# Moving stores, weight loads and mask making of a graph kernel out of the preparation of its tile tables into its first edge sum

## The reference, cut to what matters

```python
edge_index = jnp.stack([src, dst])
h = jnp.maximum(_layernorm(x), 0.0)
x = x + L0(h, edge_index, edge_weight, ...)   # weighted graph convolution and a 2-layer head
...                                           # L1: graph convolution
...                                           # L2: three typed attention layers
...                                           # L3: attention with edge attributes

def L0(h6, edge_index, edge_weight, W, b, W1, b1, W2, b2):
    row, col = edge_index                     # self-loops of weight 1 are appended to both
    deg = segment_sum(ew_sl, row_sl)
    norm = rsqrt(deg)[row_sl] * ew_sl * rsqrt(deg)[col_sl]
    msgs = (h6 @ W)[col_sl] * norm[:, None]
    h7 = segment_sum(msgs, row_sl) + b
    return relu(h7 @ W1 + b1) @ W2 + b2
```

## Time and profile before

| | us |
|---|---|
| median of 3 runs (range) | 5548.44 (5533.56 to 5564.57) |
| profiled execution, its own time | 5535.18 |
| span of the profile | 5533.5 |
| first SP issue of `load_pairs` | 174.28 |
| first SP issue of `spread_sum` | 207.99 |
| first and last start of an indirect addition (L867) | 221.1 and 1088.0 |
| first SP issue of `between_sums` | 1093.54 |

### The profile page before, as it was taken

The page is one execution under the profiler, slowest core; times in us unless marked ns, Lnnn a source line. Parts: engine busy times, 40 slices in busy tenths (PEclk is TensorE's granted clock), DMA queues, the critical chain, the costliest instruction groups (busy, mean ns, idle before and its releaser), DMA issues. The chain is left out here.

```text
span 5533.5 us, 69081 instructions
## 1 busy us (share of the span) xinstructions
PE 4208.4 (76%) x19341; PEld 3323.8 (60%) x19341; DVE 3814.4 (69%) x8692; ACT 1622.2 (29%) x3882; POOL 3333.5 (60%) x3108
## 2 busy tenths in 40 slices
PE   4666666377777678887987888798788878878886
PEld 4554445254444566666886666688666667756665
DVE  6644444275555569998436999853699986679998
ACT  3443334230000432222443222234322223422221
POOL 2388888717777467774136777513677750067775
PEclk9888888689999889998998999999899999989998
DMA  4488888736666577786027787612787762077775
GB/s 159 102 123 124 124 122 124 112 118 209 211 212 210 169 236 240 238 242 190 23 73 235 241 244 238 199 32 73 224 245 237 238 188 67 17 220 235 233 239 171
DMA packets 525140, 959.77 MB, mean 173 GB/s; under 512 B 87701, under 2 KB 299875, under 8 KB 523954
## 3 DMA queue, kind: packets, MB, share of 16 engines
q0 software_dynamic: 224512, 549.90, 39.6%
q1 hardware_dynamic: 300130, 404.93, 22.9%
q10 hardware_dynamic: 128, 0.52, 0.0%
HBM read 718.56 MB, written 236.50 MB: 173 GB/s over the span
## 5 line engine op out<-in xcount | busy, mean ns | idle before, releaser
L1462 POOL DMA_INDIRECT L2a_rows<-kv_rows,typed_index x960 | 957.8, 998 | 292.5 <-issue 292.5
L1767 PE MATMUL L2a_sums<-L2a_weighted,L2a_hot 128*128 128x264 f32 x2784 | 791.1, 430 | 204.6 <-DVE L2a_weighted L1617 174.5
L867 POOL DMA_INDIRECT sum_rows<-L0s_rows,L0s_row_of x464 | 726.8, 1566 | 153.7 <-issue 119.3
L1756 PE MATMUL L2a_query<-x,L2a_turned 128*128 x2784 | 727.9, 408 | 50.5 <-ACT L2a_turned L1711 27.8
L1767 PEld LDWEIGHTS L2a_sums<-L2a_weighted,L2a_hot 128*128 128x128 f32 x2784 | 555.3, 209 | 347.8 <-DVE L2a_weighted L1617 199.1
L1756 PEld LDWEIGHTS L2a_query<-x,L2a_turned 128*128 128x128 f32 x2784 | 568.4, 207 | 152.5 <-issue 56.5
L1286 POOL DMA_INDIRECT L1s_rows<-rows,index x464 | 451.1, 972 | 270.4 <-ACTq L87 129.2
L1462 POOL DMA_INDIRECT L3a_rows<-feature_rows,index x464 | 480.9, 1037 | 154.9 <-issue 154.9
L1002 PE MATMUL L0s_message<-features,L0s_share 128*128 x928 | 314.9, 498 | 292.4 <-ACT L0s_share L967 292.4
L1462 POOL DMA_INDIRECT hold<-kv_rows,typed_index x432 | 429.0, 993 | 178.4 <-issue 178.4
L2298 POOL TENSOR_SCALAR L2d_here<-hold,mask 128x256 f32<-128x256 f32 x200 | 183.1, 934 | 537.8 <-DVE hold L2374 389.7
(11 more groups left out here) (428 smaller groups left out, 8319.0 us busy)
## 6 DMA issues: line engine op xcount, KB each, us to landing
code_rows<-L1s_code SPq DMA_DIRECT2D x232, 256.0 KB, 2.9
L3a_code<-code_rows SPq DMA_DIRECT2D x116, 512.0 KB, 4.0
L0s_wide<-source_rows SPq DMA_DIRECT2D x116, 256.0 KB, 3.9
L2a_turn<-turned_rows SPq DMA_DIRECT2D x87, 256.0 KB, 4.4
L2a_pens<-mask_rows SPq DMA_DIRECT2D x87, 256.0 KB
L2a_hot<-hot_rows SPq DMA_DIRECT2D x87, 256.0 KB, 3.9
kv_rows<-L2d_key_rows SPq DMA_DIRECT2D x50, 384.0 KB, 2.6
kv_rows<-L2d_value_rows SPq DMA_DIRECT2D x150, 128.0 KB, 2.4
```

The lines of the kernel that those rows point to most:

```text
L867: pool.indirect_dma_start(c.sum_rows[u], bass.IndirectOffsetOnAxis(ap=row_of[:, 4 * n + u:4 * n + u + 1], axis=0), rows[n % ring][:, u, :] ...
L1462: pool.indirect_dma_start(rows[n % ring][:, u, :], None, table, bass.IndirectOffsetOnAxis(ap=index_of[:, t:t + 1], axis=0)).then_inc(lande ...
L1756: last = pe.matmul(query[q % 2][:, u, :], turned[quad % 2][:, u, :], at(c.q, b[2 * q + u // 2]), start=True, stop=True)
L1767: last = pe.matmul(sums[(m * WP + j) % held][:, :], hot[quad % 2][:, j % 2 * 2 + k, :], weighted[:, 2 * j + k, :], start=k == 0, stop=k == 1)
```

## The change

The four attribute fields are copied by GpSimd instead of ScalarE, into a free part of the accumulator `c.acc`. VectorE clips the source indices first. The key's transposes and the edges' first and last keys are only copied to `c.acc`; masks and links are made from them in `spread_sum`, after quads 4 to 8 of VectorE's loop. SyncE's loads of weights and its stores of fields follow the first eight `wide` loads of `spread_sum`, its store of masks follows quad 11, and their landing is waited for at the end of that stage.

```diff
-def load_pairs(nc, c, copies):
+def load_pairs(nc, c):
...
         def _(sp):
-            for to, source in copies:
-                sp.dma_start(to, source).then_inc(stored, 16)
             sp.wait_ge(clipped_ready, 1)
             sp.dma_start(c.source_rows...)
-            sp.wait_ge(split, 1)
-            for f in range(4):
-                sp.dma_start(c.field_rows[f, :, :]..., fields[:, f, :, :]).then_inc(stored, 16)
-            sp.wait_ge(filled, 1)
-            sp.dma_start(c.mask_rows...)
-            sp.wait_ge(stored, 16 * (6 + len(copies)))
+            sp.wait_ge(stored, 16)
...
+            dve.tensor_scalar(clipped[:, :, :], ...).then_inc(clipped_ready, 1)
             dve.tensor_copy(ends[:, 0, :], ...)
             dve.tensor_copy(ends[:, 1, :], ...)
-            dve.tensor_scalar(clipped[:, :, :], ...).then_inc(clipped_ready, 1)
-            dve.memset(masks[:, :, :, :], -FAR)
-            dve.memset(apart[:, :, :], 1.0)
-            dve.memset(c.links[:, :], 0.0)
...
-            ...  (L532 to L547: copies, four differences, five masks, links)
+            dve.tensor_copy(c.origin, origin_ps)
+            dve.tensor_copy(c.start, first_ps[:, :])
+            dve.tensor_copy(c.tail, last_ps[:, :])
+            dve.tensor_copy(c.key_t, key_ps[:, :, :])
...
         def _(act):
-            for f in range(4):
-                last = act.activation(fields[:, f, :, :], c.raw[:, :, :, 4 + f], ACT.Copy)
-            last.then_inc(split, 1)
...
+        def _(pool):
+            for f in range(4):
+                pool.tensor_copy(c.fields[:, f, :, :], c.raw[:, :, :, 4 + f])

-def spread_sum(nc, c, name):
+def spread_sum(nc, c, name, copies):
...
             for n in range(wides):
                 load_wide(n)
+            for to, source in copies:
+                sp.dma_start(to, source).then_inc(kept, 16)
+            for f in range(4):
+                sp.dma_start(c.field_rows[f, :, :]..., c.fields[:, f, :, :]).then_inc(kept, 16)
             for n in range(quads):
+                if n == 3 * ring:
+                    sp.wait_ge(masked, 1)
+                    sp.dma_start(c.mask_rows...).then_inc(kept, 16)
                 sp.wait_ge(packed, n + 1)
                 sp.dma_start(c.hot_rows[:, own], hot8[n % 2][:, :])...
...
+            sp.wait_ge(kept, 16 * (5 + len(copies)))
...
                 tally(2 * n + 1, blocks[2 * n % 8 + 1])
+                if n == 2 * ring - 4:
+                    differ_inside()         # memset of masks, one difference, two masks
+                if n == 2 * ring - 3:
+                    differ_from(2, 0)       # one difference, one mask
+                if n == 2 * ring - 2:
+                    differ_from(3, P - 1)   # one difference, one mask
+                if n == 2 * ring - 1:
+                    mark_origin()           # the fifth mask
+                if n == 2 * ring:
+                    link()                  # two memsets, two differences, links
```

More of the change, by code:

```diff
@@ L531, in _ @@
             dve.tensor_copy(c.heads[:, :], heads_ps)
[L532 to L542, removed]
-                              ALU.is_equal).then_inc(filled, 1)
-            dve.tensor_tensor(apart[:, 1:, 0], first_ps[:, 1:], tail[:, 0:NT - 1], ALU.not_equal)
-            then(dve.tensor_tensor(apart[:, :, 1], first_ps[:, :], tail[:, :], ALU.not_equal))
-            dve.tensor_scalar(c.links[:, 0:2 * NT], apart[:, :, :].rearrange("p t s -> p (t s)"), -FAR, None, ALU.mult)
-            dve.tensor_scalar(c.linked[:, :], apart[:, 0::WT, 0], -1.0, None, ALU.add)
+            dve.tensor_copy(c.origin, origin_ps)
+            dve.tensor_copy(c.start, first_ps[:, :])
+            dve.tensor_copy(c.tail, last_ps[:, :])
+            dve.tensor_copy(c.key_t, key_ps[:, :, :])
         @block.tensor
@@ L850, in spread_sum @@
         hot_stored, turn_stored = ([st.sem(f"{x}{s}") for s in range(2)] for x in ("hot_stored", "turn_stored"))
+        framed, masked, kept = (st.sem(x) for x in ("framed", "masked", "kept"))
         wide_landed = [st.sem(f"wide_landed{s}") for s in range(wides)]
@@ L933, in tally, with then, differ_inside, differ_from @@
                 dve.tensor_tensor(to, to, number[:, j:j + 1], ALU.add).then_inc(counted, 1)
+            count = [0]
+            def then(instruction):
+                count[0] += 1
+                instruction.then_inc(framed, 1)
+                dve.wait_ge(framed, count[0])
+            def differ_inside():
+                dve.memset(c.masks[:, :, :, :], -FAR)
+                then(dve.tensor_tensor(c.differ[:, :, 1:], c.key_t[:, :, 1:], c.key_t[:, :, 0:P - 1], ALU.not_equal))
+                dve.tensor_scalar(c.masks[:, :, 0, 1:], c.differ[:, :, 1:], -FAR, None, ALU.mult)
+                then(dve.tensor_scalar(c.masks[:, :, 1, 0:P - 1], c.differ[:, :, 1:], -FAR, None, ALU.mult))
+            def differ_from(k, e):
+                then(dve.tensor_tensor(c.differ, c.key_t, spread(c.key_t[:, :, e], 2, P), ALU.not_equal))
+                then(dve.tensor_scalar(c.masks[:, :, k, :], c.differ, -FAR, None, ALU.mult))
+            def mark_origin():
+                dve.tensor_tensor(c.masks[:, :, 4, :], spread(c.count[0:CH, :], 1, 4), spread(c.origin, 2, P),
+                                  ALU.is_equal).then_inc(masked, 1)
+            def link():
+                dve.memset(c.links[:, :], 0.0)
+                then(dve.memset(c.apart, 1.0))
+                dve.tensor_tensor(c.apart[:, 1:, 0], c.start[:, 1:], c.tail[:, 0:NT - 1], ALU.not_equal)
+                then(dve.tensor_tensor(c.apart[:, :, 1], c.start, c.tail, ALU.not_equal))
+                dve.tensor_scalar(c.links[:, 0:2 * NT], c.apart.rearrange("p t s -> p (t s)"), -FAR, None, ALU.mult)
+                dve.tensor_scalar(c.linked[:, :], c.apart[:, 0::WT, 0], -1.0, None, ALU.add)
             for s in range(hots):
```

37 lines of the change are left out of this document (20 added, 17 removed).

## The result

The changed kernel is slower: 5564.60 us as the median of 14 runs (5555.17 to 5576.86), against 5549.26 us for 14 runs of the kernel before. The ratio is 1.0031, with a 95% interval of 1.0020 to 1.0042, that is 17 us more by a ratio and 15 by the medians, where 12 us less was forecast. The profiled execution took 5562.49 us, its span is 5560.9.

What follows compares the result with a forecast made beforehand. The prediction took GpSimd's additions to bound the first sum and a store's landing to end the preparation. Its terms, -22.4 + 10.3 = -12.1 us, took 5548.4 to 5536.3 us, range 5514 to 5553.

Steps and rivals of the forecast that it cites:

- The preparation (-22.4 us): Stage before the first sum: ends with VectorE's copy at 185.2 us, so the sum starts 22.4 us earlier (15.9 to 22.4).
- S: Start of the first sum, at its first `wide` load: 207.99 us before, 185.6 forecast.
- as the sum had it: The prediction's total of its terms, not the kernel's stage: -22.4 + 10.3 = -12.1 us.
- Ten transfers ahead of the byte store (+10.3 us): Start of the first sum: quad 0's byte stores queue behind weights and fields, GpSimd waits 10.3 us (3.6 to 18.3).
- The masks behind quad 11 (0): First sum: the masks' store delays quad 12's byte stores, but ScalarE's lead of about three quads covers it, costing nothing.
- The starved rival: First sum: SyncE's queue starves beside additions, fields cost 18.3 us and masks 18; 14 us slower, 5562; chance 0.07.
- Masks on VectorE inside the sum (0): First sum, quads 4 to 8: some 11 us of masks and links lie under VectorE's 422.0 us of waiting, costing nothing.
- GpSimd: four copies ... hidden under VectorE: Preparation: GpSimd's four field copies take 7.3 us, end at 181.7 before VectorE, and cost nothing.
- The forecast's own test: End of the first sum: GpSimd's last addition starts some 12 us earlier; forecast wrong if under 4 or over 19.

Runs made afterwards that it cites:

- the spread versions: Changed kernel, fields on ScalarE, moved transfers issued one at a time at every second quad from quad 12: 0.9974 with stores cut into 112 and 4, 0.9994 undivided.

## Why the prediction was wrong, point by point

**The preparation (-22.4 us): the mechanism held, the size was 19.2 by S.** VectorE's copy of the keys ends the stage, as the sum had it, but ended at 188.6 and not at 185.2. Of the 3.4 us, 0.83 are an earlier stage that ended later in this execution (VectorE starts at 175.16 instead of 174.33), and 2.75 are VectorE slowed by GpSimd's copies; together a little over the 3.4. (The first addition gained 19.8, since it starts 12.5 us behind S and not 13.1.) The sum took GpSimd's copies as harmful only if they ended last. They were shorter than the 7.3 us taken (5.14), and cost more by what they did beside them.

**Ten transfers ahead of the byte store (+10.3 us): right, and 7.3 us.** GpSimd restarted at S + 27.6, not S + 31.2; the wait for the store and its place were as forecast, and 7.3 lies within the bounds of 3.6 and 18.3.

**The masks behind quad 11 (0): wrong, about 7 us.** The step counted ScalarE's lead of three quads as a cover. But each addition also waits for the one four before it, whatever ScalarE has in hand, and beside the masks additions landed after up to 10.6 us instead of 6.9. (That both meet on the masks' four engines is argued, not shown.) The starved rival had the place and a price of 18 us, but by the wrong wait, the byte stores'. Its total, 14 us slower, is close to the measured 15 by luck: it has 36 us of losses in the queue, where the runs show 14.6, and 16 from GpSimd's later transfers.

**Masks on VectorE inside the sum (0): wrong, 3.8 us.** The step asked only whether VectorE has time to spare, and it has: from quad 2 to quad 8 no gap of GpSimd was released by ScalarE, the engine that VectorE would hold up. It left out what VectorE's instructions do to GpSimd's beside them. In each of the six traces with the masks inside the sum one addition takes 3.66 to 4.43 us and ends 0.61 or 0.62 us behind the fourth mask instruction; in the seven with the masks in the preparation no addition takes more than 2.09. Over the first 36 additions the time beyond 1.55 us each is 4.5 to 5.9 us in the six and 0.7 to 1.5 in the seven. The queue is not the cause, since the spread versions show it with no moved transfer issued yet. No run moves the masks alone, and which of the four instructions holds the addition up was not told apart.

**What turned the sign: the copies' cost was confined to their stage.** Up to here the terms are -19.8 + 7.3 + 7.3 + 3.8 = -1.4 us, which the variant with the fields on ScalarE shows to be about nothing (1.0002). The other 16 us come from the step "GpSimd: four copies ... hidden under VectorE". No rival priced what an instruction does to the duration of later ones. GpSimd is the engine that sets the pace of the first sum, the attention layers and the last one, and of its 2784 gathers and additions all but the second sum's 464 got 6 to 11 ns longer by the median. With no case for it, the range ended at 5553 us, and all cases but the starved one had a gain. The 0.85 for a change of less than 0.5% came true with 0.31%, but that is the width of the bound and says nothing for the mechanism. The forecast's own test, a shift of the last addition by 4 to 19 us earlier, failed with 6.7 us later.

**Open:** why copies do this. Kind and order are shown: copies and, less, multiplications, not memsets, and only behind them. Not shown is why early copies pass over the second sum and reach the layers behind it, while copies behind the first sum reach just that second sum, nor where in GpSimd the 6 to 11 ns are spent.

## What to carry to other kernels

Before an instruction is given to an idle engine, ask what that engine does later: if thousands of its transfers pace the kernel, compare the shortest and median duration of these transfers in both traces first, since a shift of 6 to 11 ns in code that nobody touched is a cost of 16 us here. Ask also what the two engines do to each other's instructions while they overlap: idle time on VectorE did not make its masks free. A store moved beside other transfers is worth what its engines are worth: cut 116 partitions into 112 and 4, and issue the pieces where the consumers have work in hand. A lead counted in quads covers a late input, but not a transfer that waits for its own predecessor.

## What the runs showed of the hardware

- An indirect transfer's time on GpSimd depends on what GpSimd executed earlier: 1545 against 1552 ns for additions, 947 against 953 and 946 against 957 for gathers of the attention and last layers, within 2 ns in every kernel with early copies; without copies only multiplications lengthen additions (1551).
- GpSimd's copies lengthen some of VectorE's instructions beside them (a tensor-scalar operation from 0.40 to 1.19 us, a copy of 128x8 from 0.17 to 1.09), and not its copy out of PSUM (0.63, and 0.64 without GpSimd's copies) or its memset of 116x2560 (2.19 us beside the copies and without them).
- The other way round, a memset of 116x2560 and three operations of 116x508 on VectorE, some 3.5 us in all, lengthen the one addition beside them from 1.55 to between 3.66 and 4.43 us.
- A hardware queue's store that runs on four of 16 engines makes a software queue's additions land late: up to 10.6 us instead of 6.9, though both queues together use only 43.7% + 28.7% of the engines behind the masks (270 to 292 us). Cut into 112 and 4, the masks in one row still give 9.1, and one at a time 6.7. The row of that stretch in before and in after, issues with their median time to landing, in us, shows it:

```profile
sum_rows<-L0s_rows,L0s_row_of POOLq DMA_INDIRECT x12, 4.9
sum_rows<-L0s_rows,L0s_row_of POOLq DMA_INDIRECT x10, 9.6
```
